# Expert products of a decoder layer: down projections turned over into three f32r passes, their operands weighted by GpSimd and summed in PSUM

## The reference

```python
topk_idx, tw = _route(x, router_w, bias)        # 16 experts in 4 groups: best 2 groups, then best 4 experts
combine = (jax.nn.one_hot(topk_idx, E) * tw[..., None]).sum(1)      # 1024 x 16, four entries a row not zero
h = jnp.einsum('td,edf->etf', x, gate_w)        # E = 16, d = f = 128
u = jnp.einsum('td,edf->etf', x, up_w)
y = jnp.einsum('etf,efd->etd', jax.nn.silu(h) * u, down_w)
routed = jnp.einsum('etd,te->td', y, combine)
sh = jax.nn.silu(x @ sh_gate_w) * (x @ sh_up_w) @ sh_down_w         # two shared experts, always on
return routed + sh
```

## Time and profile before

| | |
|---|---|
| three runs | 203.48, 204.64, 205.24 us (median 204.64) |
| the profiled execution | 204.31 us, of which the span of instructions is 202.5 us |
| busy, of the span | PE 90%, DVE 77%, ACT 46%, POOL 38% |
| mean granted TensorE clock | 0.983 |

### The profile page before, as it was taken

The page is one execution under the profiler, slowest core; times in us unless marked ns, Lnnn a source line. Parts: engine busy times, 40 slices in busy tenths (PEclk is TensorE's granted clock), DMA queues, the critical chain, the costliest instruction groups (busy, mean ns, idle before and its releaser), DMA issues.

```text
span 202.5 us, 5182 instructions
## 1 busy us (share of the span) xinstructions
PE 181.3 (90%) x1841; PEld 146.3 (72%) x1841; DVE 156.9 (77%) x409; ACT 92.1 (46%) x181; POOL 76.5 (38%) x151
## 2 busy tenths in 40 slices
PE   5689998998998999896679599989999999999993
PEld 5478766666765467676568488878888888888883
DVE  5774686778868969898975589998877877788774
ACT  6468677776756345555533662313222232223222
POOL 4485200266874565656632222222330522220002
PEclk9999999999999999999979969999999999999999
DMA  5988000001110000000000001010100000000003
GB/s 151 320 237 233 7 3 5 5 27 29 29 29 0 3 0 0 0 3 2 0 0 0 0 5 52 26 31 0 52 26 26 26 26 0 0 0 0 0 5 104
DMA packets 10981, 7.40 MB, mean 37 GB/s; under 512 B 1665, under 2 KB 10193, under 8 KB 10833
## 3 DMA queue, kind: packets, MB, share of 16 engines
q1 hardware_dynamic: 10096, 6.80, 11.4%
q10 hardware_dynamic: 864, 0.33, 0.6%
HBM read 6.60 MB, written 0.52 MB: 35 GB/s over the span
## 4 chain that ended last, share of the span: by engine, by line
PE 59%; DVE 16%; ACT 8%; POOL 8%; issue 8%; DVEq 0%; POOLq 0%; ACTq 0%
PE banks L1425 12%; PE banks L1300 5%; PE banks L1322 4%; PE banks L1327 3%; PE banks L1323 3%; PE banks L1326 3%; PE banks L1325 3%; PE banks L1324 3%; PE banks L1130 3%; POOL kbd L393 3%; PE banks L1274 3%; DVE sum L850 2%; PE banks L1260 2%; PE banks L1245 2%; ACT vbd L567 2%
## 5 line engine op out<-in xcount | busy, mean ns | idle before, releaser
L647 ACT ACTIVATE sil<-banks 128x512 f32<-128x512 f32 x36 | 21.5, 599 | 57.1 <-PE banks L1324 57.1
L1049 DVE SCALAR_TENSOR_TENSOR x<-banks,combine,x 128x128 f32<-128x128 f32 x116 | 32.7, 345 | 8.3 <-PE banks L1425 8.0
L1425 PEld LDWEIGHTS banks<-dn_w,act 128*128 128x128 f32 x240 | 31.4, 191 | 2.8
L1425 PE MATMUL banks<-dn_w,act 128*128 (+1 forms) x240 | 31.6, 274 | 0.0
L970 DVE TENSOR_TENSOR act<-sil,banks 128x512 f32<-128x512 f32 x36 | 24.7, 686 | 5.2 <-ACT sil L647 2.2
L487 POOL TENSOR_TENSOR gu_hi<-gu_w,zero_col 128x256 fp32r<-128x256 f32 x18 | 11.0, 614 | 44.5 <-PE banks L1327 44.5
L1322 PE MATMUL banks<-x3hi,gu_lo 128*128 128x512 f32 x36 | 17.4, 482 | 1.1 <-DVE act L970 0.8
L393 POOL TENSOR_TENSOR kbd<-kbd,rs 128x1024 f32<-128x1024 f32 x7 | 13.3, 1902 | 12.5 <-DVE rs L854 12.5
L1300 PE MATMUL banks<-vo_fold,p2T 128*128 128x128 f32 x128 | 17.5, 295 | 0.3 <-ACT p2T L641 0.3
L1300 PEld LDWEIGHTS banks<-vo_fold,p2T 128*128 128x128 f32 x128 | 16.3, 207 | 0.8 <-ACT p2T L641 0.7
L401 POOL TENSOR_SCALAR ve<-mv 128x1 f32<-128x1 f32 x16 | 3.1, 196 | 32.8 <-DVE mv L752 32.4
(11 more groups left out here) (164 smaller groups left out, 372.5 us busy)
## 6 DMA issues: line engine op xcount, KB each, us to landing
wkv_sb<-in_L_xattn_w_kv_dram SPq DMA_DIRECT2D x1, 1024.0 KB, 7.3
gu_w<-in_L_ffn_gate_w_dram SPq DMA_DIRECT2D x16, 64.0 KB, 1.7
gu_w<-in_L_ffn_up_w_dram SPq DMA_DIRECT2D x16, 64.0 KB, 1.9
wq_sb<-in_L_xattn_w_q_dram SPq DMA_DIRECT2D x1, 512.0 KB, 4.6
wout_sb<-in_L_xattn_w_out_dram SPq DMA_DIRECT2D x1, 512.0 KB, 6.0
x<-in_x_dram SPq DMA_DIRECT2D x3, 128.0 KB, 3.1
out_dram<-x SPq DMA_DIRECT2D x4, 64.0 KB, 1.6
out_dram<-x ACTq DMA_DIRECT2D x4, 64.0 KB, 1.6
```

The costliest lines, as they stand in the source:

```text
L647: sc.activation(sil[:, j % 2, :], bank[2 * (j % 2)], ACT.Silu).then_inc(sil_s, 1)
L1049: dve.scalar_tensor_tensor(out=x[:, t, :], in0=bank[4 + (j + 2) % 4][:, m * D:(m + 1) * D], scalar=combine[:, t, bass.ds(e, 1)], in1=x[:, ...
L1425: last = pe.matmul(bank[4 + (j + 2) % 4][:, m * D:(m + 1) * D], act[:, j % 4, m * P:(m + 1) * P], dn_w[:, bass.ds(n, 1), :].rearrange("p o ...
```

## The change

1. `down` is turned over for 17 of the 18 experts (34 units): the down weights are the stationary operand, 512 tokens of activations stream, in three f32r passes (lo x hi, hi x lo, hi x hi). The result has features on partitions and tokens on columns, and all units of a chunk are summed in one PSUM bank (`SUM[c]`). At the end each sum is copied (`copy_sum`), turned back by four transposes (`transpose_sum`) and added to `x` (`add_sum`). The last expert (units 34 and 35) keeps the old form (`down_last`).
2. The weight of a token can no longer be a number per partition, so the activations are weighted ahead of the product. `combine` of a chunk is transposed on PE, copied by ACT to `combT` (16 partitions by 512), and for each of 30 routed units SP copies one row of it to all 128 partitions (`spread_combine`, SBUF to SBUF, 2 KB to a partition, eight buffers). POOL multiplies `act` by it in place (`scale_act`, 128x512).
3. Activations must be split: ACT rounds them (`round_act`) and the rest is taken by `rest_act`, on POOL for units 2 to 7 and on DVE for all others. PE issues `gate_up(k)` and then `down(k-3)`.
4. The down weights must be split: POOL does nine pairs (`split_down`) in steps 0 to 5 of the first attention block. The raw weights now lie in the memory of `vo_fold`, so ACT's first copy into `vo_fold` waits until all nine are split.
5. Routing is cut at tiles 0 to 3 and 4 to 7 and has some instructions fewer; units are reordered (the first chunk of experts 0 to 3 comes before their second); `act` has eight buffers; the first two `gate_up` move ahead of the last transposes of the second attention block; loops are written out; some start-up matmuls and the context fold are moved.

```diff
@@ ACT: first copy into vo_fold @@
                     if j == 0:
                         sc.wait_ge(tg_r, 1)
+                        sc.wait_ge(dsplit_lo, NE // 2)
@@ POOL @@
+            def split_down(m):
+                if m == 0:
+                    pool.wait_ge(dn_l, 48)
+                ws = slice(2 * m, min(2 * m + 2, NE - 1))
+                pool.tensor_tensor(dn_hi[:, ws, :], dn_w[:, ws, :],
+                                   zero_col[:, 0:ws.stop - ws.start].unsqueeze(2).to_broadcast([P, ws.stop - ws.start, D]),
+                                   ALU.add).then_inc(dsplit_hi, 1)
+                pool.wait_ge(dsplit_hi, m + 1)
+                pool.tensor_tensor(dn_lo[:, ws, :], dn_w[:, ws, :], dn_hi[:, ws, :].bitcast(F32),
+                                   ALU.subtract).then_inc(dsplit_lo, 1)
+            def scale_act(j):
+                k = ROUTED[j]
+                pool.wait_ge(g_s, k + 1)
+                pool.wait_ge(spread_l[j % SPREAD], 16 * (j // SPREAD + 1))
+                pool.tensor_tensor(act_of(k), act_of(k), spread[:, j % SPREAD, :], ALU.mult).then_inc(scale_s, 1)
+        DOWN_SPLITS = {0: (0, 1), 1: (2, 3), 2: (4, 5), 3: (6,), 4: (7,), 5: (8,)}
@@ SP @@
+            def spread_combine(j):
...
+                sp.dma_start(spread[:, j % SPREAD, :],
+                             combT[e:e + 1, c * CHUNK:(c + 1) * CHUNK].unsqueeze(1).to_broadcast([1, P, CHUNK])).then_inc(spread_l[j % SPREAD], 16)
@@ DVE @@
+            def rest_act(k):
+                dve.wait_ge(ahi_s, place[k] + 1)
+                dve.tensor_tensor(act_lo[:, place[k] % 3, :], act_of(k), act_hi[:, place[k] % 3, :].bitcast(F32),
+                                  ALU.subtract).then_inc(alo_s, 1)
-                    dve.scalar_tensor_tensor(out=x[:, t, :], in0=bank[4 + (j + 2) % 4][:, m * D:(m + 1) * D],
-                                             scalar=combine[:, t, bass.ds(e, 1)], in1=x[:, t, :],
-                                             op0=ALU.mult, op1=ALU.add).then_inc(acc_s, 1)
+            for k in range(15, NK - 1):
+                multiply(k)
+                rest_act(k - 2)
@@ ACT @@
+            def round_act(k):
...
+                sc.copy(act_hi[:, place[k] % 3, :], act_of(k)).then_inc(ahi_s, 1)
@@ PE @@
-                for m in range(TPC):
-                    last = pe.matmul(bank[4 + (j + 2) % 4][:, m * D:(m + 1) * D], act[:, j % 4, m * P:(m + 1) * P],
-                                     dn_w[:, bass.ds(n, 1), :].rearrange("p o d -> p (o d)"), start=True, stop=True)
+                wait_rest(pe, k)
+                pe.matmul(SUM[c], dn_lo[:, n, :], hi, start=first, stop=False)
+                pe.matmul(SUM[c], dn_hi[:, n, :], lo, start=False, stop=False)
+                pe.matmul(SUM[c], dn_hi[:, n, :], hi, start=False, stop=last).then_inc(y_s, 1)
+            for k in range(16, NK):
+                gate_up(k)
+                down(k - 3)
```

More of the change, by code:

```diff
@@ new lines, in _ @@
+                if i == 2 * NT - 2:
+                    exp_logits(early)
+            silu(0)
+            silu(1)
+            copy_p2T(NT - 2)
+            copy_x3T(NT - 3)
+            copy_p2T(NT - 1)
+            round_act(0)
+            copy_x3T(NT - 2)
+            silu(2)
+            copy_x3T(NT - 1)
+            round_act(1)
+            exp_logits(late)
+            silu(3)
+            silu(4)
+            round_act(3)
+            copy_combT(0)
+            silu(5)
+            round_act(4)
@@ new lines, in _ @@
+            silu(6)
+            round_act(2)
+            silu(7)
+            round_act(5)
+            silu(8)
+            round_act(6)
+            silu(9)
+            copy_combT(1)
+            round_act(7)
+            silu(10)
+            silu(11)
+            silu(12)
+            round_act(8)
+            silu(13)
+            round_act(9)
+            round_act(10)
+            silu(14)
+            round_act(11)
+            round_act(12)
+            for k in range(15, NK - 1):
+                silu(k)
+                round_act(k - 2)
@@ new lines, in _, with add_sum @@
+            norm_stats(2, NT - 1)
+            split_x3(NT - 2)
+            multiply(1)
+            rest_act(0)
+            multiply(2)
+            split_x3(NT - 1)
+            choose_experts(early)
+            rest_act(1)
+            expert_weights(early)
+            def add_sum(c):
+                dve.wait_ge(ysumT_s, c + 1)
+                xs = x[:, c * TPC:(c + 1) * TPC, :].rearrange("p t d -> p (t d)")
+                dve.tensor_tensor(xs, SUMT[c], xs, ALU.add).then_inc(acc_s, 1)
@@ L1090, in _, with keep_busy @@
+            rest_act(8)
+            multiply(13)
+            rest_act(9)
+            rest_act(10)
+            multiply(14)
+            rest_act(11)
+            rest_act(12)
+            for k in range(15, NK - 1):
+                multiply(k)
+                rest_act(k - 2)
+            rest_act(NS - 1)
+            multiply(NK - 1)
+            for k in range(NS, NK):
+                add_sum(chunk(k))
+                accumulate(k)
         @block.tensor
         def _(pe):
-            def keep_busy(times):
+            def keep_busy(times, where):
@@ new lines, in _ @@
+            transpose_p2(NT - 2)
+            transpose_xn3(NT - 3)
+            output2(NT - 2, 0)
+            output2(NT - 2, 1)
+            logits(NT - 3)
+            transpose_p2(NT - 1)
+            output2(NT - 1, 0)
+            output2(NT - 1, 1)
+            transpose_xn3(NT - 2)
+            gate_up(2)
+            logits(NT - 2)
+            transpose_xn3(NT - 1)
+            down(0)
+            logits(NT - 1)
+            gate_up(3)
+            gate_up(4)
+            down(1)
+            transpose_combine(0)
@@ new lines, in _ @@
+            gate_up(5)
+            down(3)
+            gate_up(6)
+            down(4)
+            gate_up(7)
+            gate_up(8)
+            down(2)
+            gate_up(9)
+            down(5)
+            transpose_combine(1)
+            gate_up(10)
+            down(6)
+            gate_up(11)
+            down(7)
+            gate_up(12)
+            gate_up(13)
+            down(8)
+            gate_up(14)
+            down(9)
+            down(10)
+            gate_up(15)
+            down(11)
```

498 lines of the change are left out of this document (271 added, 227 removed).

## The result

The changed kernel takes **428.19 us** (median of five runs, 427.65 to 429.93) against 204.64 for the kernel before (five runs beside it, 202.99 to 205.62): a ratio of 2.096, 95% interval 2.083 to 2.109. Forecast was 214.1 us with a range of 199 to 218. The forecast's last rival is what happened: the spread transfers set the pace.

The account below looks back on a forecast made before the run. PE was taken to bound the kernel before, POOL after the change. The last unit's end at 200.6, 6.2 for the end, 5.5 for ACT's stall and 1.8 around the span gave 214.1 us, range 199 to 218.

Parts of the forecast that it names:

- last rival: Spread transfers, all reading one partition, set the pace: 14.2 us each, near 550 us; 410 by the skill's figure; chance 0.05.
- From there to the end: Late routing to last unit: spread transfer 3.5 us, then POOL's pairs of 4.65 set the pace, PE done at 200.6.
- POOL, the weighting: scale_act of 128x512 on POOL takes 1.27 us, with 1.04 as the other end.
- POOL and DVE together: Two-operand SBUF instructions on POOL and DVE wait for each other: two units cost POOL 4.65 us, 3.85 without.
- PE's unit of 2.07: Three f32r passes replace the f32 down: 0.22 us less a unit, 7.5 us for 34 units.
- Late routing: DVE's late routing from 113.3 takes 15.5 us plus 9.4 lost beside POOL; late combine ready at 137.7.
- ACT waits in the first attention block: First copy into vo_fold waits for the last down split: 5.5 us later, range 4 to 7.5, not given back.
- Hand-over: Attention to experts: second chunk's operand whole at 113.3, 3.5 us earlier with 2.07 more work done, 5.5 in all.
- Hardly meet: Rival: POOL and DVE seldom meet, PE sets the pace from 130: 198.6 us; range 196 to 202, chance 0.20.
- POOL keeps up, late routing doesn't: Rival: POOL's pair is 4.05, PE sets the pace from 138.4: 207.0 us; range 205 to 209, chance 0.17.
- Smaller stall: Rival: ACT's stall is smaller or the hand-over gains more: 202 to 206 us, chance 0.08.
- slower: The changed kernel would be slower than the one before: chance 0.65.

Follow-up runs that it names:

- wide: Changed kernel with each spread reading 512 columns of all 128 partitions of wkv_sb, not one partition of combT, so wrong weights: 219.51 us.
- eight: Changed kernel, whole computation, with expert weights written eight times and each spread reading eight partitions four apart: 221.62 us, ratio to before 1.087.
- unweighted: As eight_early, without the spread transfers and POOL's 30 multiplications, so routed activations are not weighted: 199.43 us.
- act_rounds: As eight_early, with gu_hi of the last eight experts' weights rounded by ACT in place of POOL: 207.91 us, ratio to before 1.020.
- short_rest: As eight_early, but from unit 8 on DVE's rest_act computes only 8 of 512 columns: 205.74 us.
- eight_early: As eight, with all nine down splits in steps 0 and 1 of the first attention block, not 0 to 5: 213.46 us.

## Why the prediction was wrong

**The step that failed** is the transfer in "From there to the end": "between 3.1 us for 128 KB and 4.6 for 512 KB, 3.5". Both rows are loads from DRAM that write 128 partitions of SBUF, so they bound the number of bytes and not the place that they are read from. For a source of 128 partitions the price was good: 2.4 us to landing in wide. A spread reads one partition, and took 9.5 us. The sum also counts the transfer once, as a delay ahead of unit 8, and has no term for one spread following another, while POOL needed one every 2.3 us. 30 x 9.5 = 285 us from the first spread at 128 on are 413; the last weighting starts at 414.5. The Trainium skill's figure in "SBUF — State Buffer", section Door 1, gave estimates of 9.5 us and 410 us in the prediction: the trace agrees with the first, 9.47 to 9.65 us, and the total was off by 18 us. I gave the rival a chance of 0.05 because no row bore on it. But a row that doesn't bear on a thing speaks as little for 3.5 as against 9.5: the right reading was an open price from 3.5 up, a forecast with two sides, and a range to 410 and beyond. My own price of it, 14.2 us, took one engine's 18.4 GB/s for the port's; one partition gave 27.2 to sixteen engines together.

**Right, seen once the spread is mended** (wide and eight, forecast 214.1):
- "POOL, the weighting", 1.27: 1.26 after.
- "POOL and DVE together", 3.85 alone and 4.65 with meetings: 3.90 and 4.85. PE's unit of 2.07: 2.09 in unweighted. That POOL sets the pace is shown by act_rounds and short_rest.
- "Late routing": late `combine` at 137.7 by the forecast, 136.76 in act_rounds, which has no stall. Of the 9.4 us put down to meetings 6.6 came back with the operand in PSUM, 5.5 at the end; the rest isn't accounted for, but some instructions of that piece still wait there.

**Mis-sized.**
- "ACT waits in the first attention block", 5.5 us: the copy came 6.9 later in the changed kernel (54.61 - 47.71), inside the range of 4 to 7.5, and the end 8.2 by eight_early, outside it. The forecast named the lower clock after such a gap as a reason for more, but left it out of the 5.5; it cost some 1.7.
- "Hand-over" held: in act_rounds DVE's last `x3lo` ends at 112.83 (the forecast's 113.3). The words "that cancels the stall" are not a term of the sum, which goes on from 113.3 and adds the 5.5 at its end.
- The other 5.5 us, between the forecast's span of 212.3 and wide's 217.8, can be followed in wide, with the stall of 5.5 added to the forecast's times. Late `combine` is ready at 145.2 in place of 143.2. Unit 27 is weighted at 195.86 in place of 192.6; the 1.2 us that this adds to those 2.0 lie in the pairs, 4.85 for 4.65 and the first of them 5.3. Then the last split, which "is not waited for", was: unit 28's weighting starts behind it at 198.17, PE waits for that unit until 201.31, and from there runs without a gap to 211.35, where the forecast has 206.1. That is 2.0 us more, and 0.3 are in the end.

**The rivals.** "Hardly meet" (198.6) is out by wide's 4.85, and so is "POOL keeps up, late routing doesn't" (207.0), which needs a pair of 4.05. "Smaller stall" is out by 54.61. The forecast's "slower" came true, but by luck as far as the changed kernel goes: the transfers made it so. Its own reason, POOL, is true of eight and wide, and hidden in the changed kernel.

## What to carry to other kernels

Before a transfer is priced, ask which SBUF partitions it reads as well as which it writes: one partition copied to 128 went at 27 GB/s here with all sixteen DMA engines on it, and reading eight rows four apart instead removed 207 us (428.2 to 221.6). Ask too how often the kernel wants such a transfer, and not only how late the first one lands. Where no row shows a resource that a change leans on 30 times, keep both prices in the range. And a second SBUF operand on DVE can cost a whole POOL instruction when POOL is busy: moving one of the two to PSUM gave 5.5 us here.

## What the runs showed of the hardware

- Reading from SBUF by DMA: 27.2 GB/s from one partition, 25 from partitions 0 to 3, 98 from 0, 4, 8 and 12; 256 KB from 128 partitions to 128 landed in 2.4 us.
- SP's issue instruction took 9.57 us, in place of 0.43, for a load of 64 KB that had nothing to do with the slow transfers but stood behind them.
- When DVE and POOL met, the one that came second took longer: in wide POOL's splits (1.06 for 0.61, 1.25 for 0.73), in act_rounds its weightings (1.7 for 1.27), in routing DVE's instructions of 64 columns (1.13 to 1.33 for 0.22). One operand in PSUM freed DVE's two-operand instructions; a TENSOR_SCALAR with one SBUF input still took 1.27.
- After PE had stood idle for 7.16 us in eight its granted clock was 0.50 from 54.4 to 60 us, and 32 products took 2.35 us in place of 1.59; by 63 us it was back at 1.00. In the changed kernel, where PE stood idle before each unit, the clock was 0.59 from 200 to 400 us.
